# Ranks of selected queries: running sums over tiles and three matrix products in place of three chains of 32

## What is computed

```python
scores = jnp.einsum('bhqd,bhkd->bhqk', q, k) * scale
sparsity = scores.max(axis=-1) - scores.mean(axis=-1)
_, top_idx = jax.lax.top_k(sparsity, U)            # U = 307 of 4096
q_sel = jnp.take_along_axis(q, top_idx[..., None], axis=2)
attn = jax.nn.softmax(einsum('bhud,bhkd->bhuk', q_sel, k) * scale, axis=-1)
out = zeros_like(q).at[bi, hi, top_idx].set(einsum('bhuk,bhkd->bhud', attn, v))
```

## Time and profile before

| | us |
|---|---|
| runs of the kernel: lowest, median, highest of 3 | 3268.93, 3275.21, 3281.18 |
| span of the profiled execution | 3267.6 |
| PE busy (matmul ends are modelled) | 2972.6, 91% |
| DVE busy | 2890.4, 88% |
| ACT busy | 2836.5, 87% |
| POOL busy | 1580.4, 48% |

### The profile page before, as it was taken

How to read it: one execution, slowest core, us unless ns; L and a number is a source line. 1 busy time by engine, 2 the same in 40 slices (tenths; PEclk the granted TensorE clock), 3 DMA queues, 4 the chain that set the end, 5 groups by cost and what they waited for, 6 DMA issues and landing times. The chain is left out here.

```text
span 3267.6 us, 57726 instructions
## 1 busy us (share of the span) xinstructions
PE 2972.6 (91%) x15364; PEld 1367.2 (42%) x15364; DVE 2890.4 (88%) x5704; ACT 2836.5 (87%) x6246; POOL 1580.4 (48%) x2787
## 2 busy tenths in 40 slices
PE   6999899998989999998999999899999899997688
PEld 3333333333433443443334444444444343444477
DVE  4999999999989998998999999899999898997567
ACT  5999889997988999899899888799988699895566
POOL 4223122224644553654355564766565663557754
PEclk8999999999999999999999999999999999998889
DMA  6334223342151131223121233122151023202022
GB/s 182 90 86 121 76 71 81 90 34 40 34 38 31 35 41 17 32 40 35 24 41 30 60 52 40 36 39 41 37 48 41 24 39 32 41 15 16 16 83 73
DMA packets 263603, 163.56 MB, mean 50 GB/s; under 512 B 168876, under 2 KB 242796, under 8 KB 259180
## 3 DMA queue, kind: packets, MB, share of 16 engines
q1 hardware_dynamic: 255180, 156.41, 25.8%
q0 software_dynamic: 6144, 1.37, 0.5%
q10 hardware_dynamic: 1952, 2.10, 0.2%
HBM read 111.86 MB, written 47.86 MB: 49 GB/s over the span
## 5 line engine op out<-in xcount | busy, mean ns | idle before, releaser
L1189 DVE CUSTOM_DVE_ANT_0 JK<-DP,AB 128x1024 bf16<-128x1024 f32 x2048 | 2463.1, 1222 | 239.8 <-DVE SPr L1189 91.5
L1033 ACT ACTIVATE AB<-CP 128x512 f32<-128x512 f32 x4096 | 2291.3, 622 | 201.0 <-PE CP L749 147.0
L768 PE MATMUL DP<-KS,QS 128*128 128x512 f16 x4096 | 1230.2, 382 | 61.5 <-DVE SPr L1189 53.9
L1641 POOL TENSOR_TENSOR SCR<-E 128x307 f16<-128x307 f32 x957 | 666.1, 709 | 516.3 <-ACT E L1068 509.2
L749 PE MATMUL CP<-KS,QS 128*128 128x512 f16 x2048 | 789.7, 386 | 57.4 <-ACT AB L1033 34.6
L758 PE MATMUL CP<-KS,QS 128*128 128x512 f16 x2048 | 790.4, 386 | 34.8
L768 PEld LDWEIGHTS DP<-KS,QS 128*128 128x128 f16 x4096 | 357.0, 99 | 357.9 <-DVE SPr L1189 171.5
L1068 ACT ACTIVATE E<-BP 128x307 f32<-128x307 f32 x904 | 430.5, 476 | 34.5 <-PE BP L860 31.3
L749 PEld LDWEIGHTS CP<-KS,QS 128*128 128x128 f16 x2048 | 197.5, 96 | 525.3 <-ACT AB L1033 460.3
L758 PEld LDWEIGHTS CP<-KS,QS 128*128 128x128 f16 x2048 | 196.8, 96 | 411.5 <-ACT AB L1033 376.2
L860 PE MATMUL BP<-QT,KA 128*128 128x307 f16 x904 | 267.2, 296 | 22.6 <-ACT QT L1060 19.0
(11 more groups left out here) (414 smaller groups left out, 3087.2 us busy)
## 6 DMA issues: line engine op xcount, KB each, us to landing
KS<-KTC SPq DMA_DIRECT2D x256, 128.0 KB, 4.6
QS<-QSC SPq DMA_DIRECT2D x512, 64.0 KB, 2.2
KA<-KTC SPq DMA_DIRECT2D x128, 128.0 KB, 4.0
QN<-SCR SPq DMA_DIRECT2D x16, 544.0 KB, 3.4
SCR<-in_L_attn_x SPq DMA_DIRECT2D x16, 512.0 KB, 5.0
AO<-E SPq DMA_DIRECT2D x16, 512.0 KB, 6.9
VF<-in_L_attn_x SPq DMA_DIRECT2D x64, 128.0 KB, 2.2
VF<-AO SPq DMA_DIRECT2D x64, 128.0 KB, 2.2
```

What stands on the lines that cost most here:

```text
L768: r = pe.matmul(o[:, 512 * j:512 * j + 512], qs, ks[j][:, 0, :], start=True, stop=True)
L1033: act.activation(AB[p % 3][:, 512 * j:512 * j + 512], BANK["C%d" % j], ACT.Abs).then_inc(ab_full, 1)
L1189: dve.tensor_tensor_reduce(out=JK[p % 2][:], in0=BANK["D%d" % u], in1=AB[p % 3][:], scale=1.0, scalar=0.0, op0=ALU.add, op1=ALU.max, accum ...
L1641: pool.tensor_tensor(EL[a % NE], E[a % NE][:], EH[a % NE], ALU.subtract).then_inc(el_g, 1)
```

## The change

The two masks are kept interleaved, mask 1 and mask 2 of a tile side by side, behind a tile of zeros (`marks`, in masks12). Five shifted additions (`cum`, i = 0 to 4, shifts of 1, 2, 4, 8 and 16 tiles, in two buffers that alternate, with 16 tiles of zeros ahead) make the running sum over tiles of both masks at once. GpSimd does them in the main loop, VectorE in the tail. `rank` is then three products: triangular on the masks, all-ones on the running sums shifted by one tile, and all-ones on the last running sum of mask 1, which gives the count. VectorE makes `need`, the minimum of it and the rank among "equal", the comparison, and the sum with the rank among "greater". `pick` (GpSimd in the main loop, VectorE in the tail) builds the chosen mask and multiplies. The main-loop order is now `cut`, 2 idle steps, 5 `cum`, 1 idle, `rank`, 1 idle, `pick`, 2 idle, `slots`. ONE_BANK holds flip, cut, rank and idx. GpSimd also sets the zero tiles for each group at `cut`.

```diff
@@ -28,12 +28,12 @@
 NE = 10
 PVLAG = 6
 HEAD0 = [sum(n for _, _, n in GROUPS[:g]) for g in range(len(GROUPS) + 1)]
-SEL0 = [22 * g for g in range(len(GROUPS))]
+SEL0 = [20 * g for g in range(len(GROUPS))]
 NP = 2 * NT
 XW = 4 * 128 + 16
-ONE_BANK = ("flip", "cut", "need", "rank1", "rank2", "idx")
+ONE_BANK = ("flip", "cut", "rank", "idx")
 
 
 def after(engine, semaphore, value):
@@ -210,13 +210,18 @@
         for _ in range(2 * gaps):
             yield []
         yield [("cut", g, bank())]
-        for _ in range(3 * gaps):
+        for _ in range(2 * gaps):
             yield []
-        yield [("need", g, bank())]
-        yield [("rank1", g, bank())]
-        for _ in range(4 * gaps):
+        for i in range(5):
+            yield [("cum", g, i, "D" if tail[0] else "G")]
+        for _ in range(gaps):
             yield []
-        yield [("rank2", g, bank())]
+        yield [("rank", g, bank())]
+        for _ in range(gaps):
+            yield []
+        yield [("pick", g, "D" if tail[0] else "G")]
+        for _ in range(2 * gaps):
+            yield []
         yield [("slots", g)]
         for _ in range(3 * gaps):
             yield []
...
         masks12 = sb("masks12", [128, 512], BF16)
-        msk, msk2 = (masks12[:, 256 * i:256 * i + 256].rearrange("p (t h) -> p t h", h=8) for i in range(2))
+        running = lower_half[:].bitcast(BF16)
         msk3 = sb("msk3", [128, NT, HM], BF16)
         counted = sb("counted", [128, 1])
...
@@ -632,6 +637,27 @@
 
             return NJ * NQ * GROUPS[g][2]
 
+        def marks(g):
+
+            n = GROUPS[g][2]
+            return masks12[:, 0:(NT + 1) * 2 * n].rearrange("p (t m h) -> p t m h", m=2, h=n)
+
+        def sums(g, i):
+
+            w = (16 + NT) * 2 * GROUPS[g][2]
+            return running[:, w * i:w * i + w].rearrange("p (t m h) -> p t m h", m=2, h=GROUPS[g][2])
+
+        def picked(g):
+
+            return msk3[:].rearrange("p t h -> p (t h)")[:, 0:NT * GROUPS[g][2]].rearrange("p (t h) -> p t h", h=GROUPS[g][2])
+
+        def summand(g, i):
+
+            if i == 0:
+                return marks(g)[:, 1:NT + 1], marks(g)[:, 0:NT]
+            v = sums(g, (i - 1) % 2)
+            return v[:, 16:16 + NT], v[:, 16 - (1 << i):16 - (1 << i) + NT]
+
         def group_of(n):
             return next(g for g in range(len(GROUPS)) if HEAD0[g] <= n < HEAD0[g + 1])
...
-                owed[bank] = ((sel_m, 5 * g + 2),)
-
-            def masks(g):
-                n = GROUPS[g][2]
-                return [m[:].rearrange("p t h -> p (t h)")[:, 0:NT * n].rearrange("p (t h) -> p t h", h=n)
-                        for m in (msk, msk2, msk3)]
-
-            def need_(g, bank):
-                n = GROUPS[g][2]
+                owed[bank] = ((sel_m, 4 * g + 2),)
+
+            def rank(g, bank):
+                w = 2 * GROUPS[g][2]
                 o = claim(bank)
-                pe.wait_ge(sel_m, 5 * g + 1)
-                for j in range(NT):
-                    i = pe.matmul(o[:, 0:n], onesb[:], masks(g)[0][:, j, :], start=j == 0, stop=j == NT - 1)
-                i.then_inc(sel_pe, 1)
-                owed[bank] = ((sel_m, 5 * g + 3),)
-
-            def prefix(g, o, m):
-                n = GROUPS[g][2]
-                pe.matmul(o[:, 0:NT * n], trib[:], m, start=True, stop=False)
-                for t in range(NT - 1):
-                    i = pe.matmul(o[:, (t + 1) * n:NT * n], onesb[:],
-                                  m[:, t:t + 1, :].broadcast_to([128, NT - 1 - t, n]), start=False, stop=t == NT - 2)
-                return i
-
-            def rank1(g, bank):
-                o = claim(bank)
-                pe.wait_ge(sel_m, 5 * g + 2)
-                prefix(g, o, masks(g)[1]).then_inc(sel_pe, 1)
-                owed[bank] = ((sel_m, 5 * g + 4),)
-
-            def rank2(g, bank):
-                o = claim(bank)
-                pe.wait_ge(sel_m, 5 * g + 4)
-                prefix(g, o, masks(g)[2]).then_inc(sel_pe, 1)
-                owed[bank] = ((sel_m, 5 * g + 5),)
+                m, r = (v.rearrange("p t m h -> p (t m h)") for v in (marks(g), sums(g, 0)))
+                pe.wait_ge(sel_m, 4 * g + 2)
+                pe.matmul(o[:, 0:NT * w], trib[:], m[:, w:(NT + 1) * w], start=True, stop=False)
+                pe.wait_ge(sel_cum, 5 * g + 5)
+                pe.matmul(o[:, w:NT * w], onesb[:], r[:, 16 * w:(15 + NT) * w], start=False, stop=True)
+                pe.matmul(o[:, NT * w:NT * w + w // 2], onesb[:], r[:, (15 + NT) * w:(15 + NT) * w + w // 2], start=True,
+                          stop=True).then_inc(sel_pe, 1)
+                owed[bank] = ((sel_m, 4 * g + 3),)
 
             def idx(g, bank):
...
+
+            def rank(g, bank):
+                n, sf = GROUPS[g][2], views(g)[0].rearrange("p (t h) -> p t h", h=GROUPS[g][2])
+                p1, p2 = (BANK[bank][:, 0:2 * NT * n].rearrange("p (t m h) -> p t m h", m=2, h=n)[:, :, m, :]
+                          for m in range(2))
+                bound = need[:, 0:n].unsqueeze(1).broadcast_to([128, NT, n])
                 dve.wait_ge(sel_pe, SEL0[g] + 19)
-                dve.tensor_scalar(need[:, 0:n], BANK[bank][:, 0:n], -1.0, float(U), ALU.mult, ALU.add).then_inc(sel_m, 1)
-
-            def rank1(g, bank):
-                n, _, (m1, m2, m3, *_) = views(g)
-                dve.wait_ge(sel_m, 5 * g + 3)
-                dve.wait_ge(sel_pe, SEL0[g] + 20)
-                q = seq.mark(dve.tensor_tensor(m3, BANK[bank][:, 0:NT * n].rearrange("p (t h) -> p t h", h=n),
-                                               need[:, 0:n].unsqueeze(1).broadcast_to([128, NT, n]), ALU.is_le))
+                q = seq.mark(dve.tensor_scalar(need[:, 0:n], BANK[bank][:, 2 * NT * n:2 * NT * n + n], -1.0, float(U),
+                                               ALU.mult, ALU.add))
                 dve.wait_ge(q_dve, q)
-                q = seq.mark(dve.tensor_tensor(m3, m3, m2, ALU.mult))
+                q = seq.mark(dve.tensor_tensor(sf, p2, bound, ALU.min))
+                dve.tensor_tensor(picked(g), p2, bound, ALU.is_le)
                 dve.wait_ge(q_dve, q)
-                dve.tensor_tensor(m3, m3, m1, ALU.add).then_inc(sel_m, 1)
-
-            def rank2(g, bank):
-                n, (_, _, m3f, sf, *_), _ = views(g)
-                dve.wait_ge(sel_pe, SEL0[g] + 21)
-                dve.tensor_tensor(sf, BANK[bank][:, 0:NT * n], m3f, ALU.mult).then_inc(sel_m, 1)
+                dve.tensor_tensor(sf, p1, sf, ALU.add).then_inc(sel_m, 1)
+
+            def pick(g, on):
+                if on == "D":
+                    m, sf = picked(g), views(g)[0].rearrange("p (t h) -> p t h", h=GROUPS[g][2])
+                    dve.wait_ge(sel_m, 4 * g + 3)
+                    q = seq.mark(dve.tensor_tensor(m, m, marks(g)[:, 1:NT + 1, 1, :], ALU.mult))
+                    dve.wait_ge(q_dve, q)
+                    q = seq.mark(dve.tensor_tensor(m, m, marks(g)[:, 1:NT + 1, 0, :], ALU.add))
+                    dve.wait_ge(q_dve, q)
+                    dve.tensor_tensor(sf, sf, m, ALU.mult).then_inc(sel_m, 1)
 
             def slots(g):
-                n, (_, _, _, sf, si, bi), _ = views(g)
-                dve.wait_ge(sel_m, 5 * g + 5)
+                sf, si, bi = views(g)
+                dve.wait_ge(sel_m, 4 * g + 4)
                 after(dve, sel_f, g)
...
 
+            def cut(g, bank):
+                w = 2 * GROUPS[g][2]
+                pool.wait_ge(sel_thr, g + 1)
+                pool.memset(marks(g)[:, 0:1].rearrange("p t m h -> p (t m h)"), 0.0)
+                for i in range(2):
+                    r = pool.memset(sums(g, i)[:, 0:16].rearrange("p t m h -> p (t m h)"), 0.0)
+                r.then_inc(sel_pad, 1)
+
+            def cum(g, i, on):
+                if on == "G":
+                    if i == 0:
+                        pool.wait_ge(sel_pad, g + 1)
+                        pool.wait_ge(sel_m, 4 * g + 2)
+                    else:
+                        pool.wait_ge(sel_cum, 5 * g + i)
+                    pool.tensor_tensor(sums(g, i % 2)[:, 16:16 + NT], *summand(g, i), ALU.add).then_inc(sel_cum, 1)
+
+            def pick(g, on):
+                if on == "G":
+                    n = GROUPS[g][2]
+                    m, sf = picked(g), slotf[:].rearrange("p t h -> p (t h)")[:, 0:NT * n].rearrange("p (t h) -> p t h", h=n)
+                    pool.wait_ge(sel_m, 4 * g + 3)
+                    pool.wait_ge(q_pool, seq.mark(pool.tensor_tensor(m, m, marks(g)[:, 1:NT + 1, 1, :], ALU.mult)))
+                    pool.wait_ge(q_pool, seq.mark(pool.tensor_tensor(m, m, marks(g)[:, 1:NT + 1, 0, :], ALU.add)))
+                    pool.tensor_tensor(sf, sf, m, ALU.mult).then_inc(sel_m, 1)
+
             def slots(g):
                 n = GROUPS[g][2]
```

40 lines of the change are left out of this document (22 added, 18 removed).

## The result

| us | kernel before | changed kernel |
|---|---|---|
| lowest, median, highest of 4 runs each, on one chip | 3268.77, 3272.07, 3281.18 | 3246.63, 3250.50, 3254.29 |
| span of the profiled execution | 3267.6 | 3246.8 |

The ratio is 0.9933 (95% interval 0.9913 to 0.9953): 0.7% faster. On a second chip, six more runs of the changed kernel had a median of 3252.47 and a ratio of 0.9926 (0.9906 to 0.9947). I had forecast 3267.7 with a range from 3256 to 3278, so the prediction was wrong: three times as much came back as I had worked out.

A forecast was written before the change was run, and what follows sets the result against it. VectorE's L1189 was taken to bound the main loop, the selection chain the tail. Main loop -14.4 + 4.0 + 1.5 = -8.9, tail +1.4: -7.5 on 3267.6 gives 3260.1, plus 7.6 makes 3267.7 us, range 3256 to 3278.

The forecast's parts named there:

- steps that move: Six steps of attention move from the tail into the main loop at 0.25 us each, +1.5 us.
- Chains: Main loop: need, rank1 and rank2 products are paid in full, 3.7 us per 5-head group, 2.7 per 3-head group.
- What comes in their place: Main loop: VectorE's four operations in `rank` and two short waits cost 1.3 us (5 heads) or 1.1 (3 heads).
- GpSimd's lateness: Main loop: TensorE's `rank` waits for GpSimd's fifth `cum`, 4.0 us together, 3.4 in group 4; bounds nothing and 12.
- The tail's small work: Tail, group 7: `cut` to `slots` 1.6 us shorter, less 0.8 for VectorE's four small operations of otr.
- `put` ahead of the copies: Tail: GpSimd does 4.26 us of `put` before copies fa and fb, so the chain stands 2.9 us.
- the EL: Tail: an EL of 0.7 us no longer stands in front of the one-hot products, -0.7 us.
- From span to median: Whole kernel: the runs' median lies 7.6 us above the profiled span, carried over to the forecast.
- Rival 1: GpSimd nowhere late, `put` not delaying the copies: -15.2 up to -19 us, 3256 to 3260; chance 0.2.
- Rivals 2 and 3: 2: TensorE waits for GpSimd everywhere, 3276, chance 0.2. 3: GpSimd additions cost over about 1.3 us, 3288, chance 0.06.

The follow-up runs named there:

- fourth experiment: Kernel before, chains kept, with need and rank1 no longer holding back steps of attention: 3288.21 us, ratio 1.0038.
- third: Changed kernel with the first three cum steps of each group held free of attention and feed-forward: 3254.57 us, ratio 0.9941.
- fifth experiment: Changed kernel with no attention step handed out beside cum, rank, pick and slots in the tail: 3246.64 us, ratio 0.9908.
- eighth experiment: Kernel before with group 6's next gathers at key tile 2 instead of 10, arrangement at 12 instead of 18: 3271.59 us, ratio 0.9982.
- twelfth experiment: Changed kernel with GpSimd making each cum addition of the main loop twice: 3272.35 us, ratio 0.9985.
- second experiment: Changed kernel with VectorE making cum and pick in the main loop too: 3256.84 us, ratio 0.9937.

## Why the prediction was wrong, step by step

On the spans I forecast -7.5 us and found -20.8. The stages give -13.4 for the main loop (forecast -8.9) and -4.3 for the tail (forecast +1.4); the remaining 3.1 us are the first row of the table. Two steps of the prediction failed: "steps that move" was priced at +1.5 us for six steps of attention and left out what the others leave behind, some 9 us the other way; and the digits of the tail stood at nothing, where the trace has -4.9.

- **Chains.** Forecast 22.9 us before VectorE's part is taken off (4 x 3.7 + 3 x 2.7), measured 23.3 in the trace and 23.3 by doubling them. Right in the sum, with some luck in the parts: group 0, which I had taken to look like group 1, has 4.7, and group 5 has 3.2.
- **What comes in their place.** Forecast 1.3 and 1.1 us in `rank`, measured 0.9 (2.05 - 1.15) in groups of 5 and 0.7 in group 3 (a step of 1.84). I had added up durations; operations without a true wait between them start 0.2 to 0.25 us apart. 5.7 us for seven groups instead of 8.5: 2.8 us too much. This is why no `rank` step is 2.3 to 2.5 us long as I had asked for: they are 2.05, 2.05, 3.81, 1.84, 2.89, 2.05 and 4.75.
- **GpSimd's lateness.** Forecast 4.0 us, nearly all in group 4; measured 7.0, in groups 6, 2 and 4. In group 4 the ten operations of f5 turned out to lie behind the last addition, not ahead of it (it ends at 2025.6, TensorE waits 1.29 us). What I had missed was `put`: I had asked what it is queued ahead of in the tail, not in the main loop. The term was within its bounds, its places were not.
- **The DMA at group 0.** Missed, +6.3 us. The new order puts `slots` and with it the index DMAs three steps later in every group, while group 0's attention starts only one step later: in the kernel before its gathers stood back four steps behind the index DMAs, until the projection of the values was planned, and now they stand back two. I had worked out that group 0's attention starts one step later, and took a step for a time.
- **Steps that move.** Here lies the largest error. I put the 6 attention steps that come into the main loop at +1.5 us and stopped. But a group's selection is now three steps longer, and 12 of its 16 steps go with attention or feed-forward where 6 of 13 did; 21 steps leave the stretches between the selections, and all later work falls on other steps. By difference this costs 3.1 us in the selections (-7.5 against -23.3 + 5.7 + 7.0), and the excess elsewhere falls by 11.9 without group 0's 6.3 (by 10 to 14, depending on which traces are compared and with the stretch ahead of group 0's `cut` left out). Of that, 5 us are 21 steps at the mean excess of 0.24 us of the stretches that they leave. Another 5 us lie in one place, steps 1764 to 1796, where group 5's first gathers meet the end of the feed-forward. GpSimd and VectorE before, then VectorE in the changed kernel:

```profile
2557.32 1.10 POOL L1614 DMA_INDIRECT SCR<-QN,idxs  x1 [5.82 <-DMA idxs<-IDX]
```
```profile
2568.15 1.22 DVE L1189 CUSTOM_DVE_ANT_0 JK<-DP,AB 128x1024 bf16<-128x1024 f32 x1 [5.70 <-PE DP L768]
```
```profile
2557.83 1.22 DVE L1193 CUSTOM_DVE_ANT_0 JK<-DP,AB 128x1024 bf16<-128x1024 f32 x1 [3.09 <-PE DP L794]
```

  GpSimd stands 5.82 us for the indices, and the feed-forward work that TensorE needs is queued behind; in the changed kernel it stands 1.06. The excess of these 32 steps is 19.7 us before and 14.7 after, and the experiments show what decides it: 15.0 in the kernel before with fewer held steps (fourth experiment), 18.6 in the changed kernel with three more held (third); 19.2 and 20.4 in the two other traces of a kernel before with its held steps, 14.6 to 15.4 in the other traces of the changed kernel and its variants. It goes with the held steps, not with the chains. What is left, some 2 us, is no more than the traces differ by. Why such a step is cheaper beside a `cum` than beside a digit is argued only: a digit also takes VectorE, a `cum` takes GpSimd alone.
- **The tail's small work.** Forecast -0.8 for `cut` to `slots` with otr in it, measured -0.9 and -0.3 in the two traces; +2.9 for `put` ahead of the copies, measured +2.4; -0.7 for the EL, measured -0.5. Together +1.0 to +1.6 against +1.4. The fifth experiment takes `put` out of the way, and its trace gives 2.9 us back between `slots` and fb and 1.2 between `cut` and `slots`.
- **The tail's digits.** Missed, -4.9 us. I counted that 58 instead of 64 attention steps were left and used this for the place of `put` alone. A step that is moved takes its gathers and its arrangement with it, and the eighth experiment gives 4.1 us for these, 3.2 of them in the one instruction L1216.
- **From span to median.** I carried 7.6 us over. Outside the span lie only 1.8 us (3248.58 for a span of 3246.8); the rest was that the profiled execution was a quick one. The changed kernel's median lies 3.7 us over its first profiled span.

Rival 1 (more comes back) was on the right side and still too small: it knew neither of what the moved steps leave behind nor of the gathers, and what it did name (GpSimd nowhere late, `put` out of the way) did not happen. Rivals 2 and 3 priced GpSimd's lateness; the twelfth experiment bears out their mechanism, at additions of 1.5 us rather than 1, and their premise was not met. By the Trainium skill, page "SBUF — State Buffer", section "Who interferes with whom", L1193 was to be untouched by GpSimd's additions, and it is, at 1222 ns. The Trainium skill, page "GPSIMD Engine Reference", section "Key points", has VectorE about twice as fast in elementwise work, and here 0.32 us stand against 0.72; the second experiment, with a ratio of 0.9937 against 0.9933 and 0.9926, shows that this decides little here, where VectorE is the bound.
